# Loading the adjacency, the bias and the two gates from ScalarE's DMA queue

## What is computed

```python
# layer 0
W = adj * adj
x = layernorm(x + einsum('bnf,nm->bmf', x, W) + bias)
# layer 1, h = x, causal_mask = adj
z_l, z_g, v = h @ W_lang.T, h @ W_grav.T, h @ W_V.T
A_l = relu(cosine similarities of z_l) * not_eye
A_g = exp(-squared distances of z_g / (2 * exp(log_sigma)**2)) * not_eye
K_l, K_g = rows of (A * causal_mask), each divided by its sum
w_l = sigmoid(gate_logit)
K = w_l * K_l + (1 - w_l) * K_g
x = layernorm(x + (K @ v) @ W_O.T)
```

## Time and profile before

| what | value |
|---|---|
| median of 3 runs | 680.73 us (680.61 to 681.36) |
| the profiled execution | 681.37 us |
| its span | 679.6 us |
| TensorE (PE) busy | 666.4 us, 98% |
| VectorE (DVE) busy | 506.5 us, 75% |
| ScalarE (ACT) busy | 345.6 us, 51% |
| GpSimd (POOL) busy | 210.9 us, 31% |
| DMA queues with data | one, 38.05 MB, 15.1% of 16 engines' span |

### The profile page before, as it was taken

One profiled execution on the slowest core, in us unless ns is written; L12 is line 12 of the kernel. 1 busy time (PEld: TensorE's weight loads), 2 busy tenths in 40 slices (PEclk: granted clock), 3 DMA queues, 4 the chain that ended last, 5 costly groups with the idle time before them and its releaser, 6 DMA issues.

```text
span 679.6 us, 11745 instructions
## 1 busy us (share of the span) xinstructions
PE 666.4 (98%) x3579; PEld 570.7 (84%) x3579; DVE 506.5 (75%) x1523; ACT 345.6 (51%) x614; POOL 210.9 (31%) x454
## 2 busy tenths in 40 slices
PE   8999999999999999999999999999999999999994
PEld 7888888888888888888888888889888888988883
DVE  5935696868869686886959687695968869596886
ACT  4734445464454546455454745545464554545433
POOL 0222315151341515134151513316051432502122
PEclk9999999999999999999999999999999999999997
DMA  7301102011110201111020111102011110001002
GB/s 271 118 6 58 62 32 95 1 62 63 57 68 31 93 0 62 61 62 62 31 93 0 65 58 62 62 31 93 0 69 54 62 62 31 32 0 63 1 31 94
DMA packets 20406, 38.33 MB, mean 56 GB/s; under 512 B 1824, under 2 KB 1824, under 8 KB 20384
## 3 DMA queue, kind: packets, MB, share of 16 engines
q1 hardware_dynamic: 20384, 38.05, 15.1%
HBM read 21.27 MB, written 16.78 MB: 56 GB/s over the span
## 4 chain that ended last, share of the span: by engine, by line
PE 96%; DVE 1%; DMA 1%; ACT 1%; SPq 0%; issue 0%; POOL 0%; POOLq 0%; DVEq 0%
PE ring L357 58%; PE bank_p L377 13%; PE ring L475 4%; PE bank_x L318 3%; PE bank_p L318 3%; PE bank_r L421 3%; PE bank_k L421 3%; PE bank_pt L390 2%; PE bank_r L336 1%; PE bank_pt L336 1%; PE bank_k L336 1%; PE bank_r L397 1%; DMA w_raw<-in_L_gnn_W_lang_dram 1%; PE bank_pt L408 1%; PE bank_x L336 1%; PE bank_x L377 0%
## 5 line engine op out<-in xcount | busy, mean ns | idle before, releaser
L562 ACT ACTIVATE yT_hi<-ring 128x512 fp32r<-128x512 f32 x128 | 76.0, 594 | 109.7 <-PE ring L357 109.5
L357 PE MATMUL ring<-hT_hi,T_hi 128*128 128x512 f32 x320 | 129.2, 404 | 0.0
L357 PE MATMUL ring<-hT_hi,T_lo 128*128 128x512 f32 x320 | 125.3, 392 | 0.0
L357 PE MATMUL ring<-hT_lo,T_hi 128*128 128x512 f32 x320 | 124.8, 390 | 0.0
L777 DVE TENSOR_TENSOR yT_lo<-ring,yT_hi 128x512 fp32r<-128x512 f32 x128 | 87.5, 684 | 31.4 <-ACT yT_hi L562 31.4
L357 PE MATMUL ring<-M_hi,hT_hi 128*128 128x512 f32 x256 | 101.5, 396 | 0.0
L357 PE MATMUL ring<-M_hi,hT_lo 128*128 128x512 f32 x256 | 100.2, 392 | 0.0
L357 PE MATMUL ring<-M_lo,hT_hi 128*128 128x512 f32 x256 | 99.9, 390 | 0.0
L1084 POOL TENSOR_SCALAR z_ve<-z_mv 128x2 f32<-128x2 f32 x32 | 7.0, 219 | 264.8 <-DVE z_mv L873 260.1
L1077 POOL TENSOR_TENSOR x_lo<-x_sb,x_hi 128x512 fp32r<-128x512 f32 x60 | 75.8, 1298 | 22.3 <-ACT x_hi L562 22.3
L777 DVE TENSOR_TENSOR u_lo<-ring,u_hi 128x512 fp32r<-128x512 f32 x64 | 44.3, 692 | 49.1 <-ACT u_hi L562 49.0
(11 more groups left out here) (159 smaller groups left out, 1373.8 us busy)
## 6 DMA issues: line engine op xcount, KB each, us to landing
x_sb<-in_x_dram SPq DMA_DIRECT2D x15, 1024.0 KB, 5.4
out_dram<-o_sb SPq DMA_DIRECT2D x60, 256.0 KB, 2.0
x_sb<-in_x_dram SPq DMA_DIRECT2D x2, 512.0 KB, 5.4
w_raw<-in_L_gnn_W_lang_dram SPq DMA_DIRECT2D x1, 1024.0 KB, 6.6
o_sb<-in_L_gnn_W_grav_dram SPq DMA_DIRECT2D x1, 1024.0 KB, 9.5
h_sb<-in_L_gnn_W_V_dram SPq DMA_DIRECT2D x1, 1024.0 KB, 11.7
w_raw<-in_L_gnn_W_O_dram SPq DMA_DIRECT2D x1, 1024.0 KB, 8.3
out_dram<-x_sb SPq DMA_DIRECT2D x4, 256.0 KB, 2.0
```

What stands on the lines that cost most here:

```text
L357: last = pe.matmul(bank[:, :], a, b, start=n == 0, stop=n == len(terms) - 1)
L562: return act.activation(dst, src, ACT.Copy, scale=scale)
```

## The change

The wait for the cleared tile and the five transfers of adj (two), the bias and the two gates leave SP's program and are put at the head of ScalarE's, ahead of its first copy, in the same order among themselves. What SP keeps stays in its order. Nothing that is computed changes, and the semaphores and those who wait for them are the same.

```diff
         @block.sync
         def _(sp):
             sp.dma_start(x_sb[:, 0:2, :], x_v[0][:, 0:2, :]).then_inc(x0_loaded[0], 16)
-            sp.wait_ge(adj_zeroed, 1)
-            for b in range(2):
-                s = slice(b * N, (b + 1) * N)
-                sp.dma_start(adj_bd[s, s], adj).then_inc(adj_loaded, 16)
             sp.dma_start(w_raw[0][:, :, :], w_lang.rearrange("(c p) d -> p c d", p=R)).then_inc(w_loaded[0], 16)
-            sp.dma_start(bias_bc[:, :], bias.partition_broadcast(R)).then_inc(bias_loaded, 16)
             sp.dma_start(x_sb[:, 2:4, :], x_v[0][:, 2:4, :]).then_inc(x0_loaded[1], 16)
-            sp.dma_start(gates[:, 0:1], gate_logit.partition_broadcast(R)).then_inc(gates_loaded, 16)
-            sp.dma_start(gates[:, 1:2], log_sigma.partition_broadcast(R)).then_inc(gates_loaded, 16)
             for i, w in ((1, w_grav), (2, w_v)):
                 sp.dma_start(w_raw[i][:, :, :], w.rearrange("(c p) d -> p c d", p=R)).then_inc(w_loaded[i], 16)
...
+            act.wait_ge(adj_zeroed, 1)
+            for b in range(2):
+                s = slice(b * N, (b + 1) * N)
+                act.dma_start(adj_bd[s, s], adj).then_inc(adj_loaded, 16)
+            act.dma_start(bias_bc[:, :], bias.partition_broadcast(R)).then_inc(bias_loaded, 16)
+            act.dma_start(gates[:, 0:1], gate_logit.partition_broadcast(R)).then_inc(gates_loaded, 16)
+            act.dma_start(gates[:, 1:2], log_sigma.partition_broadcast(R)).then_inc(gates_loaded, 16)
             split_x0(0)
             hi_weight(0)
             split_x0(1)
```

## The result

The changed kernel takes 683.06 us (median of 18 executions, 681.46 to 684.65) against 680.76 for the kernel before (17 of its 18 executions lie at 680.61 to 681.36, one took 1073.44); the ratio is 1.0028 with a 95% interval of 1.0021 to 1.0036. It is slower by 0.28%, or 2.3 us. 679.6 was forecast, with a range to 681.3. The eighteen executions fall into two groups: six at 681.46 to 681.82 with a mean granted TensorE clock of 0.995 or 0.996, and twelve at 682.75 to 684.65 with 0.991 to 0.994. The profiled execution is of the first group: 681.55 us, span 679.8.

What follows compares the result with a forecast made beforehand. TensorE, busy 98% of the span, bounds the kernel; only the loop's start can move. w_lang, issued 1.22 us sooner, brings the first setup matmul from 10.49 to 9.35: 680.73 - 1.15 = 679.6 us, range 678.9 to 681.3.

Steps and rivals of the forecast that it cites:

- the 7.8 that I took: Opening, SP's queue: w_lang lands at 7.8 us instead of 9.06, counting the bias's 0.7 us in full.
- early bound: Opening: w_lang's earliest landing, 7.1 us, from data starting at 3.5, 2.87 of transfer and 0.7 of completion.
- costly-issue rival: Opening, ScalarE: its issues cost more than SP's and delay the first x copy; middle 681.3 us, chance 0.12.
- the case that I had put at 5.9: Opening, ScalarE: the table load comes after the five issues, so the first x copy starts at 5.9 us.
- when adj arrives: Opening: adj, on ScalarE's queue, lets VectorE start mix at 5.5 us, bounds 4.5 to 6.1.
- path (d): Opening, TensorE: with x_lo at 6.6 us, the two layer-0 products (1.64 us) end at 9.1, before the first setup matmul.
- path (c): Opening, VectorE: from adj's arrival through x_lo, mask and first weight split, the first setup matmul can start at 8.9 us.
- contention: Opening: w_lang shares the engines with bias, adj and gates and lands at 8.4 to 9.4; middle 680.5 us, chance 0.20.
- my start at 9.35: Opening, TensorE: the first setup matmul starts at 9.35 us instead of 10.49, a gain of 1.15 us.

Runs made afterwards that it cites:

- 49 transposes: The changed kernel with 49 warm-up transposes on TensorE in place of 27: 681.88 us, ratio 1.0012.
- the experiment with the same order of issue: Kernel before, with only the two adj transfers issued on ScalarE and SP waiting for both issues before w_lang: 680.81 us, ratio 0.9999.
- adj alone on ScalarE: Kernel before, with only the adj wait and two adj transfers moved to ScalarE; bias and gates stay on SP: 683.98 us, ratio 1.0048.
- bias and gates alone: Kernel before, with only the bias and the gates moved to ScalarE; adj stays on SP: 683.72 us, ratio 1.0037.
- bias beside w_lang: Kernel before, with adj, adj and the bias on ScalarE, SP issuing w_lang after both adj issues, gates on SP: 684.32 us.
- x's second half first: The changed kernel with x's second half issued ahead of w_lang on SP: 686.01 us, ratio 1.0073.
- w_lang held back: The changed kernel with SP issuing w_lang only after ScalarE has issued both adj transfers: 685.72 us, ratio 1.0062.
- gates beside w_lang: Kernel before, with adj, adj and the gates on ScalarE, SP issuing w_lang after both adj issues, bias on SP: 683.56 us.

## Why the prediction was wrong

What held. The place was right: the opening alone decides, and the loop didn't change. SP's issue of w_lang at 1.23 was right. Its landing was at or ahead of the 7.8 that I took: by its use 7.3 in the changed kernel's trace, near my early bound of 7.1, and 7.77 in the trace with 49 transposes, where the transfers are the same. ScalarE's issues cost 1.25 + 0.60 + 0.50 + 0.69 = 3.04 us against 3.43, and the first copy came at 5.43 instead of 5.8; the costly-issue rival had no part in it. The table load moved behind the issues, the case that I had put at 5.9.

The step that failed is "when adj arrives". I gave 5.5 with a bound of 6.1 (3.2 + 2.9); mix started at 7.43. adj was even issued sooner than I had it, at 0.96 instead of 2.0, and still came later. The term that was wrong is the 2.9 us from the end of the second issue to the landing: it measured 5.2 (2.21 to 7.40). I had taken the wait that adj has today, which is that behind x's first half, and didn't count that in the new order of issue (x at 0.73, adj at 0.96, w_lang at 1.23, adj at 1.60) the 1 MB of w_lang stands ahead of the second adj transfer. I had written that in its own queue adj need not stand behind the others. It did, and the experiment with the same order of issue, beside adj alone on ScalarE, shows that this is what delays it; why a transfer on one queue waits for one on the other stays open. The rest of the path was sound: x_lo at 8.55 plus my 0.83 is 9.38, where layer 0 started, and the first setup matmul followed it without a pause at 10.86. That is path (d), through TensorE's own layer 0. On path (c) the first low part of w_lang was ready a little before that, 0.70 after the start of this row, at 10.66:

```profile
9.96 2.49 DVE L947 TENSOR_TENSOR yT_lo<-w_raw,yT_hi 128x512 fp32r<-128x512 f32 x4
```

The rival that I named contention had the right cause in general, but put the damage on w_lang; it fell on adj, which got no rival and no chance of its own. This step alone takes the time out of the range: the first group, with the clock held, starts at 681.46, and with 49 transposes the kernel takes 681.88, against an upper end of 681.3.

The second failure is the clock. In the trace of the kernel before TensorE goes from the warm-up into layer 0 with hardly a pause, from about 7.1 to 7.24:

```profile
1.66 5.47 PE L483 MATMUL bank_r<-ident 128*128 128x128 f32 x27 [1.66 <-POOL ident L1128]
```

My path (d) moved layer 0 by 0.2 us and had no idle time there, so I didn't ask what an idle TensorE costs. When layer 0 moved by 2.1 us, the gap became 2.94, and most executions took 1.7 us more at a lower mean clock. In the medians this is 1.2 to 1.5 us of the 2.3: by the two groups 683.06 less some 681.6, by the warm-up experiment, which takes it away, 683.06 less 681.88.

The length of the gap doesn't decide by itself. In single traces, idle times of 2.44 us (adj alone), 2.63 (bias and gates alone), 3.82 (bias beside w_lang), 3.91 (x's second half first) and 4.00 (w_lang held back) had a stretch at 0.50 with them or right behind them, while 2.94 (the changed kernel) and 3.04 (gates beside w_lang) had the clock at 1.00 throughout.

The third is one of bookkeeping. The profiled execution stood 0.64 us above the median, and I subtracted from the median a gain measured on that execution. Its excess lay in the very transfer that the gain was made of: an execution at the median should start the setup near 9.9 and not at 10.49, so even my start at 9.35 would have been worth some 0.5 us and not 1.15.

Of the Trainium skill's two sentences in the prediction, the one from "DMA: Bandwidth & Descriptors", section "Issuing engines are not separate DMA queues", agrees with the runs in that a second issuer gains little: adj on the second queue with the order of issue kept is worth 0.0 us (0.9999). That such transfers interleave is true of the bias and the gates, and did not hold for the second adj transfer in the stretch from 4.5 to 5.5 us, in which none of its packets moved. Of what the Trainium skill states in "DMA: Bandwidth & Descriptors", section "Queues, rings and completion order", on increments that wait across queues, no run here shows anything, since adj's data itself was late.

## What to carry to other kernels

Before a small transfer is moved to another engine's queue, list all issues of both queues by their time: what counted here was what had been issued just ahead of it, on whichever queue, and a small transfer that somebody waits for belongs ahead of the large one. When a step on the chain is hurried, work out also what happens to TensorE's idle times in front of it, because a new gap of 2 to 3 us can cost the clock for the next few us (1.7 us in twelve of eighteen executions here). And a gain should be taken against an execution near the median, above all where the profiled one is off by as much as the gain; splitting the large transfer that is waited for gained 1.0 us with the order of issue left alone. What w_lang's earlier issue would gain with adj unharmed no kernel here measures.

## What the runs showed of the hardware

- A 16 KB transfer on ScalarE's queue issued behind a 1 MB transfer on SP's landed 5.8 us after its issue (at 7.40 us of the span); on the same queue but ahead of the 1 MB, in four kernels, it was there at 4.6 to 5.75 us.
- Transfers of 1 KB in all, made of 4-byte pieces, on the second queue lengthened a 1 MB transfer beside them from 6.64 to 8.51 us, as much as 256 KB of bias did (8.36); both together made it 9.30. One trace each; in the four traces with nothing issued behind adj on the other queue ahead of its landing it took 5.99 to 6.67 us.
- After TensorE idled 2.44 us the granted clock was 0.50 and products of 512 columns went at 0.43 us each instead of 0.23; with 2.94 and 3.04 us in two other kernels' traces it was still 1.00. Twelve of eighteen executions of the changed kernel were of the slower kind.
- ScalarE's issues in the changed kernel took 0.50 to 0.69 us each (SP's there 0.44 to 0.65), and its table load came behind them, at 4.13 instead of 0.73 us.
